# Four graph-attention layers on one core: two single-head products as three rounded matmuls, exponentials in place, one output slot, another order of the queues

## What is computed

```python
h = maximum(layernorm(x), 0); x = x + L0(h, adj, W, a1, a2)   # elu(softmax(mask(leaky(f1 + f2^T))) @ h), f from h W^T a
h = maximum(layernorm(x), 0); x = x + L1(adj, h, W1, ..., W2, ...)
#   L1a: 4 heads of 256: xl = h W1; softmax over sources; attn @ xl; elu
#   L1b: 1 head of 512: xl2 = g W2; out = attn @ xl2 + b2
h = maximum(layernorm(x), 0); x = x + L2(h, adj, w_src, w_dst, b)  # softmax(mask(leaky(s_i + t_j + b))) @ h, one head
h = maximum(layernorm(x), 0); x = x + L3(h, adj, W_proj, ...)      # 8 heads of 64: relu(attn @ (h W_proj))
```

## Time and profile before

| | |
|---|---|
| median of 3 runs | 3084.61 us (3081.1 to 3087.44) |
| profiled execution | 3083.84 us, span 3082.1 us |
| mean TensorE clock granted | 0.977 |
| instructions | 79166 |
| HBM read, written | 314.93 MB, 35.59 MB |

### The profile page before, as it was taken

The page is one execution under the profiler, slowest core; times in us unless marked ns, Lnnn a source line. Parts: engine busy times, 40 slices in busy tenths (PEclk is TensorE's granted clock), DMA queues, the critical chain, the costliest instruction groups (busy, mean ns, idle before and its releaser), DMA issues. The chain is left out here.

```text
span 3082.1 us, 79166 instructions
## 1 busy us (share of the span) xinstructions
PE 2976.9 (97%) x21040; PEld 2746.1 (89%) x21040; DVE 2480.0 (80%) x8101; ACT 2319.9 (75%) x6433; POOL 2263.2 (73%) x3214
## 2 busy tenths in 40 slices
PE   7899999999999999999999999999999999999974
PEld 5789999999999999999999999999999999999964
DVE  3578888888888888888888888888888888888852
ACT  2567787778877788777787778877788777787752
POOL 3467777777777777777777777777777777777753
PEclk6999999999999999999999999999999999999985
DMA  5123333333333333333333333333333333333332
GB/s 195 34 69 123 117 119 122 108 124 118 119 123 106 125 117 119 122 109 122 118 119 121 108 122 120 120 118 112 121 120 119 118 110 122 120 120 119 96 107 93
DMA packets 205558, 355.71 MB, mean 115 GB/s; under 512 B 51904, under 2 KB 117568, under 8 KB 188736
## 3 DMA queue, kind: packets, MB, share of 16 engines
q1 hardware_dynamic: 205120, 350.66, 34.8%
HBM read 314.93 MB, written 35.59 MB: 114 GB/s over the span
## 5 line engine op out<-in xcount | busy, mean ns | idle before, releaser
L1454 POOL TENSOR_SCALAR rs<-mv,rs 128x1 f32<-128x1 f32 x512 | 357.6, 698 | 109.2 <-POOL rs L1451 108.8
L997 ACT ACTIVATE eT<-eT,tc 128x128 f32<-128x128 f32 x1024 | 314.1, 389 | 161.3 <-POOL eT L1534 161.3
L432 PE MATMUL bank_b<-w_hi,hT_hi 128*128 128x344 f32 x1536 | 419.8, 328 | 5.6 <-DVE g L1277 3.8
L432 PE MATMUL bank_c<-w_hi,g_hi 128*128 128x258 f32 x2048 | 414.1, 283 | 4.7 <-DVE x L1204 4.7
L432 PE MATMUL bank_c<-w_lo,g_hi 128*128 128x258 f32 x2048 | 414.5, 284 | 0.0
L432 PE MATMUL bank_b<-w_lo,hT_hi 128*128 128x344 f32 x1536 | 408.2, 320 | 0.0
L1329 DVE CUSTOM_DVE_ANT_0 t_all_L<-t_all_L,mask 128x128 f32<-128x128 f32 x1024 | 368.6, 413 | 27.0 <-DMA t_all_L<-t_dram_L 26.5
L432 PE MATMUL bank_b<-w_hi,hT_lo 128*128 128x344 f32 x1536 | 357.0, 327 | 0.0
L432 PE MATMUL bank_c<-w_hi,g_lo 128*128 128x258 f32 x2048 | 351.8, 284 | 0.0
L432 PE MATMUL bank_e<-w_hi,hT_hi 128*128 128x264 f32 x1024 | 341.1, 347 | 5.5 <-DVE out_sb L1372 5.4
L1540 POOL TENSOR_TENSOR eT<-eT,shift_all 128x512 f32<-128x512 f32 x256 | 331.1, 1294 | 4.6 <-ACT eT L997 4.4
(11 more groups left out here) (158 smaller groups left out, 8577.5 us busy)
## 6 DMA issues: line engine op xcount, KB each, us to landing
shift_all<-shift_dram SPq DMA_DIRECT2D x128, 1024.0 KB, 5.3
t_all_L<-t_dram_L SPq DMA_DIRECT2D x128, 512.0 KB, 3.7
x_in<-in_x SPq DMA_DIRECT2D x128, 256.0 KB, 2.6
t_all_L1a<-t_dram_L1a SPq DMA_DIRECT2D x128, 256.0 KB, 3.2
out<-out_sb SPq DMA_DIRECT2D x128, 256.0 KB, 3.1
t_all_L<-t_dram_L SPq DMA_DIRECT2D x256, 64.0 KB, 3.1
adj_in<-in_adj SPq DMA_DIRECT2D x128, 64.0 KB, 3.0
t_dram_L1a<-t_rows_L1a SPq DMA_DIRECT2D x512, 0.5 KB
```

Source lines behind the costliest of these rows:

```text
L432: last = mm(bank[:, 0:width], a[:, c * P:(c + 1) * P], w[:, c, b * width:(b + 1) * width], start=(first and c == chunks[0] and n == 0), st ...
L997: last = activation(eT[:, k, :], eT[:, k, :], ACT.Prelu, bias=tc3[:, k:k + 1], alpha=SLOPE)
L1454: ts(b, mv[layer][:, 0:1], r, -1.0, ALU.mult, ALU.mult).then_inc(sem(f"rs_made{layer}"), 1)
```

## The change

- Layers 1b and 2: the transposed exponentials and the values are split into high and low parts (new tiles pT_lo, v_hi, v_lo), and the product is three fp32r matmuls into the same bank. New stages: v_hi_L1b and v_hi_L2 on ScalarE, pT_lo_L1b, v_lo_L1b and pT_lo_L2 on VectorE, v_lo_L2 on GpSimd. Layer 0's product stays as it was.
- `p1 = e1`: the exponentials overwrite the scores. exp no longer waits for the transposition before; masked now waits for it instead of for exp.
- One output slot instead of two, one `product` tile pair for layers 0 and 2 (with a wait between them), one semaphore fewer for the statistics, one for the identity.
- The lists of all five queues are written anew, lags renamed by where the round begins (SKEW 12 to 11).

```diff
-SKEW = 12
+SKEW = 11
-        XR, MR, LR, TR, X1R, X2R, X3R, OR = 3, 10, 8, 4, 3, 2, 4, 2
+        XR, MR, LR, TR, X1R, X2R, X3R, OR = 3, 10, 8, 4, 3, 2, 4, 1
-        p1 = {k: sb(f"p_{k}", [P, P]) for k in one}
-        pT1 = {k: sb(f"pT_{k}", [P, P]) for k in one}
+        p1 = e1
+        split = ("L1b", "L2")
+        pT1 = {k: sb(f"pT_{k}", [P, P], F32R if k in split else F32) for k in one}
+        pT1_lo = {k: sb(f"pT_lo_{k}", [P, P], F32R) for k in split}
+        v_hi = {k: sb(f"v_hi_{k}", [P, D], F32R) for k in split}
+        v_lo = {k: sb(f"v_lo_{k}", [P, D], F32R) for k in split}
...
+            def product_of_parts(key, bank):
+                for n, (a, v) in enumerate(((pT1[key], v_hi[key]), (pT1[key], v_lo[key]), (pT1_lo[key], v_hi[key]))):
+                    last = mm(bank, a[:], v[:], start=(n == 0), stop=(n == 2))
+                last.then_inc(sem(f"{key}_out"), 1)
...
             def product_L1b(t, g):
                 if g.live:
-                    pe.wait_ge(sem("L1b_pT"), g.made())
+                    pe.wait_ge(sem("L1b_pT_lo"), g.made())
+                    pe.wait_ge(sem("L1b_v_lo"), g.made())
...
-                    mm(bank_c[:, 1, :], pT1["L1b"][:], xl2[:, 0:D], start=True, stop=True).then_inc(sem("L1b_out"), 1)
+                    product_of_parts("L1b", bank_c[:, 1, :])
...
             def turn_mask_L3(t, g):
...
                     if t.full:
-                        pe.wait_ge(sem("mask_copied"), g.made(-7))
+                        pe.wait_ge(sem("x3_made"), g.made(-2))
...
             def exp_one(key, g):
                 act.wait_ge(sem(f"{key}_max"), g.made())
-                act.wait_ge(sem(f"{key}_turned"), g.made(1))
...
             def masked_one(key, g, m):
                 pool.wait_ge(sem(f"{key}_spread"), 16 * g.made())
-                pool.wait_ge(sem(f"{key}_exp"), g.made(1))
+                pool.wait_ge(sem(f"{key}_turned"), g.made(1))
...
-            dve.wait_ge(sem("ident_loaded"), 16)
+            dve.wait_ge(sem("att_in"), 64)
...
             def score_columns(layer, g):
+                dve.wait_ge(sem(f"st_made{2 - layer}"), columns_issued[2 - layer])
+                columns_issued[layer] += 1
```

The new stages (those of layer 2 are alike, but v_lo_L2 runs on GpSimd and pT_lo_L2 reads bank_a):

```diff
+            def v_hi_L1b(g):                                  # ScalarE
+                    act.wait_ge(sem("xl2_made"), g.made())
+                    act.wait_ge(sem("L1b_out"), g.made(1))
+                    activation(v_hi["L1b"][:], xl2[:, 0:D], ACT.Copy).then_inc(sem("L1b_v_hi"), 1)
+            def pT_lo_L1b(g):                                 # VectorE
+                    dve.wait_ge(sem("L1b_pT"), g.made())
+                    dve.wait_ge(sem("L1b_out"), g.made(1))
+                    tt(pT1_lo["L1b"][:], bank_c[:, 0, 0:P], pT1["L1b"][:].bitcast(F32), ALU.subtract).then_inc(sem("L1b_pT_lo"), 1)
+            def v_lo_L1b(g):                                  # VectorE
+                    tt(v_lo["L1b"][:], xl2[:, 0:D], v_hi["L1b"][:].bitcast(F32), ALU.subtract).then_inc(sem("L1b_v_lo"), 1)
```

More of the change, by code:

```diff
@@ L357, in _ @@
                 load(t.graph(0))
-                store(t.graph(12))
-                spread_L2(t.graph(7))
+                spread_shift_L3(t.graph(10))
+                spread_L1b(t.graph(5))
                 send_L0(t.later_graph(2))
                 spread_L0(t.later_graph(2))
[L362 to L365, removed]
                 send_L1a(t.graph(3))
+                send_L3(t.graph(9))
                 spread_L1a(t.graph(3))
-                send_L3(t.graph(9))
                 send_L2(t.graph(6))
                 spread_L3(t.graph(9))
+                spread_L2(t.graph(6))
+                store(t.graph(11))
+                send_shift_L3(t.graph(9))
+                send_L1b(t.graph(4))
             for s in range(OR):
@@ L1144, in score_columns @@
                                                        (t_row, 0.0, targets[layer][:, 0:1]))):
-                    last = nc.vector.tensor_tensor_reduce(product[:, layer + i, :], h[layer][:], row[layer][:], 1.0, first,
+                    last = nc.vector.tensor_tensor_reduce(product[:, i, :], h[layer][:], row[layer][:], 1.0, first,
                                                           ALU.mult, ALU.add, col)
@@ L1436, in _ @@
                 residual_L1b(t.graph(5))
+                stats_3(t.graph(7))
+                targets_L3(t.graph(9))
+                recip_L0(t.later_graph(2))
+                sources_L3(t.graph(9))
+                residual_L0(t.later_graph(2))
+                stats_1(t.graph(2))
+                moments_1(t.graph(2))
+                moments_0(t.later_graph(0))
+                most_L1a(t.graph(3))
+                most_L3_first(t.graph(9))
+                most_L3_last(t.graph(9))
+                recip_L1a(t.graph(3))
+                most_leaky_L3(t.graph(9))
+                rows_shift_L3(t.graph(9))
+                stats_2(t.graph(5))
+                most_L2(t.graph(6))
+                rows_L1b(t.graph(4))
+                values_L1b(t.graph(4))
+                moments_3(t.graph(7))
+                moments_2(t.graph(5))
+                hT_lo_L3(t.graph(8))
         @block.gpsimd
@@ L1466, in scale_3, with v_lo_L2 @@
                 scale_and_bias(3, g)
+            def v_lo_L2(g):
+                if g.live:
+                    pool.wait_ge(sem("L2_v_hi"), g.made())
+                    pool.wait_ge(sem("L2_out"), g.made(1))
+                    tt(v_lo["L2"][:], h[2][:], v_hi["L2"][:].bitcast(F32), ALU.subtract).then_inc(sem("L2_v_lo"), 1)
             def make_mask(g):
```

213 lines of the change are left out of this document (113 added, 100 removed).

## The result

The kernel after takes 3376.8 us (4 runs, 3365.79 to 3383.85), the kernel before, run beside it, 3082.86 (4 runs). The ratio is 1.0949 [1.0911, 1.0987]: 294 us slower, where the prediction had 38 faster. The profiled execution took 3382.44 us.

A forecast was written before the change was run, and what follows sets the result against it. TensorE, busy 998 of 1000 us mid-loop, was taken to bound the kernel. Products -43.5, waits +19 and the end -14 gave -38 us: from 3083.84 to 3045.3 us (3046 on the median), range 3015 to 3095.

The forecast's parts named there:

- The products: TensorE, layers 1b and 2: three rounded matmuls at 0.69 us replace one of 0.86, saving 43.5 us over 128 rounds.
- What is added to the other engines: New stages add 1.25 us a round on VectorE, 1.24 ScalarE, 1.29 GpSimd; hidden under TensorE, first-order cost nothing.
- Removed waits and buffers: In-place exponentials, one output slot, shared product tile and SP's reordered transfers: all charged zero in the loop.
- Where the cover is thin: TensorE's waits at turn_mask_L3, product_L1b and product_L0: 0.15 us a round (bounds 0 and 0.6), 19 us given back.
- One engine can hold up another: VectorE scans beside GpSimd's prob_L1a: new order saves most of 0.88 us a round; signs left inside the 0.15 us.
- The end: Last rounds, bound by layer 3's chain: targets_L3 and sources_L3 ahead of the scans gain 0 to 27.5 us, 14 taken.
- Rival 3: VectorE late to residual_L2, held 0.88 us by GpSimd; turn_mask_L3 waits 0.8 us a round: slower, 3129 us; chance 0.16.

The follow-up runs named there:

- e7: Kernel after with its order and memory changes, but both products single true fp32 and without the six added stages: 3382.88 us, 1.0963.
- e10: Kernel before's queue lists with the six added stages, both products in three rounded matmuls and the kernel after's memory: 3130.21 us, 1.0158.
- e9: Kernel before with the memory changes alone (exponentials in place, one output slot, two product tiles), product_L2 in its old place: 3095.03 us, 1.0041.
- e8: Kernel before with the memory changes alone, but product_L2 one place later on TensorE, behind project_L3_last_low: 3159.69 us, 1.0241.
- e3: Kernel before with only spread_shift_L3 moved ahead of spread_L1b in SP's list: one run, 3233.39 us.
- e11: Kernel after, nothing moved, but from the second graph on the broadcast of layer 3's shift fetches 256 KB in place of 1024: 3149.66 us, 1.0226.
- e1: Kernel after with spread_shift_L3 moved on SP behind spread_L1b, send_L0 and spread_L0: 3421.4 us, 1.1102.
- e14: Kernel before with one edit, targets_L3 ahead of sources_L3 and the first four scans on VectorE: 3084.06 us, 1.0008.
- e15: Kernel after with spread_shift_L3 issued by ScalarE, behind v_hi_L1b, in place of SP: 3200.52 us, 1.0381.
- e2: Kernel after with spread_L1b alone moved ahead of spread_shift_L3 on SP, send_L0 and spread_L0 staying behind it: one run, 3523.86 us.
- e16: Kernel before with product_L1b alone in three rounded matmuls and the exponentials in place; product_L2 stays true fp32: 3096.29 us, 1.0054.

## Why the prediction was wrong

**The products.** Right. 0.68 us for three against the 0.69 worked out, 0.17 a product.

**What is added to the other engines.** Right in size, over 1500 to 2000 in the kernel after (columns as in the earlier trace rows):

```profile
L1532 POOL TENSOR_TENSOR v_lo_L<-h,v_hi_L 128x512 fp32r<-128x512 f32 x20 | 25.6, 1280 | 0.0
...
L1291 DVE TENSOR_TENSOR v_lo_L1b<-xl,v_hi_L1b 128x512 fp32r<-128x512 f32 x19 | 13.0, 682 | 0.0
...
L924 ACT ACTIVATE v_hi_L1b<-xl 128x512 fp32r<-128x512 f32 x20 | 12.4, 622 | 0.0
```

VectorE came to 797 x 25.16 / 1000 = 20.1 us a round, near the 20.4. In the new order all this cost no more than the cheaper products gave: e7, with true products and none of the added stages, takes as long as the kernel after. In the old order products and stages together were a loss (e10 against e9, 35 us): there, e8 and e9 say, the round was already set by two chains of about one length.

**Removed waits and buffers: the step that failed.** The prediction said of SP's queue: "In the loop each of these transfers is asked for several us before its reader's turn; I charge zero." I had looked at when each transfer is asked for, not at what goes out ahead of it. L1b's broadcast, 0.47 us behind 1024 KB, lands after 6.5 us in place of 3.1. e3 prices the swap at 150 us in the kernel before (a later issue included), e11 gives 227 of the 294 us back by the size of the big transfer alone, and e7 shows that the order with the memory changes makes the whole loss. The memory changes were charged zero too; e9 puts them at 13 us together. Which of them it is was not told apart.

**Where the cover is thin.** The charge of 0.15 us a round (bounds 0 and 0.6) measured 2.55, and the clock that such waits bring down, up to 0.27 us more, had no term. The places named were half right: product_L1b waits for pT_lo_L1b, 95.4 us on the matmul's own row, but because the exponentials came late, and turn_mask_L3 hardly waits (waits of the kernel after, 400 to 3100):

```profile
PE bank_a L755 <- DVE x L1242: 0.5, 2, 0.2
```

pT_L0 behind the eight leaky_L3 was the right suspicion; it showed only when the first circle was opened (e1, 1.8 us a round). The upper bound of 0.6 was taken from short waits inside an engine's row and had no transfer in it.

**One engine can hold up another.** Right. The scans of the kernel after, 500 to 2700, no longer meet prob_L1a; compare the 1165 of the earlier trace rows:

```profile
L1386 DVE CUSTOM_DVE_ANT_0 t_all_L<-t_all_L,mask x704: 279/289/519, 505.9 to 2699.1; 128x128 f32<-128x128 f32 x176
```

It gained nothing, since VectorE was not what the round waited for.

**The end.** Wrong: 14 us were taken, and from the last product_L0 on the kernel after is 3 us shorter. The wait of the earlier trace rows did fall, from 27.5 to 7.8 us, but product_L3 waits for its exponentials as it did before (18.0 us there). In the last 183 us of the kernel after:

```profile
PE bank_e L761 <- ACT eT L1036: 19.8, 6, 12.9
```

e14 has the edit alone: no change. In a round of its end targets_L3 waits 3.9 us for the leaky_L3, which the prediction had as its objection and had not counted.

**Rivals.** Rival 3 had the right sign and the wrong mechanism: VectorE was not late to residual_L2. Its 3129 us and the range's end at 3095 were both bounded by waits of under a microsecond.

Open: e11 is still 68 us above the kernel before. In it masked_L0 waits 159.9 us for L0's broadcast, whose send also stands behind the shift; that this is all of it was not tried. What the order costs when L1b goes out a full microsecond ahead of the shift, with L0's transfers ahead of it too and SP not held, was not tried either.

## What to carry to other kernels

When a queue of transfers is reordered, write down for each small one what goes out ahead of it and when that lands, what follows it within a microsecond, and what the queue waits for before it: here a small transfer just behind a big one landed with it (the kernel after, e11, e15), one 0.5 us ahead of it was late too (e2), and one behind a send was issued late (e3). A kernel whose bounding engine is 99.8% busy can have a second circle of the same length, and then shortening the first gained nothing here (e16), while a delay in the second cost its full size (e8): follow one round backwards from each short wait before pricing a saving. Moving a reader means moving its transfers too.

## What was not expected of the hardware

A 64 KB transfer issued within 0.7 us behind a broadcast of 1024 or 256 KB landed within 0.7 us of it: in the kernel after (6.5 us from its issue, the big one 6.7), in e11 (4.2 and 4.0) and, from another engine's queue, in e15 (5.1 and 5.4). The Trainium skill, "DMA: Bandwidth & Descriptors", section "Queues, rings and completion order", says that a transfer's semaphore increment lands only after every earlier write of that DMA engine, across its queues. These rows agree, but the rule does not give e2, where the small one was issued 0.50 us ahead of the big one and still took 6.0 us. Its section "Issuing engines are not separate DMA queues" says that issuing from several engines saves only the time of the sequencer, usually small beside the transfer. Here it took 176 us off 3377: SP's list, with that time and the place among the loads, lay on the circle. How much of the 176 us is the sequencer's time was not told apart.
